# Two last stages of a graph and expert kernel become one: finding the picked rows and the last expert network, with a place of its own for every gathered tile

## The chip, the cores and the metric

The kernel runs on one core of a Trainium2 chip. The time is device time in microseconds (us) of one execution of the whole program; lower is better.

## The reference

The program runs two layers (graph convolution, attention mixing, expert network) over 12500 nodes of 256 features in float32. What matters here is the last step of the second layer. A router gives every node one number; the 6249 nodes with the largest numbers are picked, and only for them a two-layer network is computed, scaled by the router's number and added to x:

```
weights = (jnp.einsum('bsd,do->bso', x, wr) + br)[..., 0]
_, idx = jax.lax.top_k(weights, k)
sel_idx = idx[:, :kk]
sel = jnp.take_along_axis(x, sel_idx[:, :, None], axis=1)
h = jax.nn.gelu(jnp.einsum('bkd,dh->bkh', sel, w1) + b1)
y = jnp.einsum('bkh,hd->bkd', h, w2) + b2
w_sel = jnp.take_along_axis(weights, sel_idx, axis=1)
y = y * w_sel[..., None]
processed = jnp.zeros_like(x).at[batch_idx, sel_idx].set(y)
return processed + x
```

`w1` is 256 x 1024 and `w2` 1024 x 256. The order of the picked nodes doesn't matter, since the result goes back to each node's own row.

## The kernel before, in words

Every stage is a function with its own semaphores and buffers, and a barrier of all engines at its end. There is no scheduler: each engine's instructions run in the order in which the code writes them, and semaphores join the engines. The last four stages are `normalize` (norm3), `select`, `pick_rows` and `ffn1`.

`norm3` writes, for each node, a row of 512 numbers to `pick_from` in HBM: the normalized x, and the x to which the result is added. `select` finds which nodes are picked (`g.picked`, a 128 x 100 map of 0 and 1) and their numbers (`g.gain`), while SyncE stores x itself to the output; it waits for that store before it ends.

`pick_rows` makes the list. The picked nodes are numbered 0 to 6248, in 49 tiles of 128 (`PICK_TILES`). TensorE counts how many are picked ahead of each column (`ps_a`, `ps_s`). For each tile, VectorE marks which column holds each of its 128 numbers (`mark`, four portions at `CUTS`: 13, 12, 12 and 12 tiles), TensorE fetches that column's running counts, gains and base by a product (`ps_rows`, six banks), and VectorE turns them into the row number and the gain (`find`: compare and sum, copy, multiply). At the end one addition writes `g.pick_row` for all tiles, and one reduction over 49 x 128 numbers writes `g.pick_gain`.

`ffn1` works on 25 groups of two tiles (`GROUP`, `ROWS` = 256 rows). For each tile GpSimd (POOL) gathers 128 rows of 512 numbers with one indirect DMA (`gather`, `rows`, six buffers, `LOADS`), and writes 128 result rows of 256 to the output with another (`scatter`, from `y`, six buffers). TensorE's order is written out: `turn(gi + 1)` (four transposes of the next group into `ps_t`), the first product of group gi (16 float32 matmuls, shown as 32 passes, into the four banks `ps_h`), then `last(gi - 1)` (two times eight float32 matmuls and one bias matmul into `ps_f`, line 3159). ScalarE applies the gelu into `ht`, VectorE copies the turned tiles to `xt` (`keep_turned`) and adds (`add`). The gather of tile t waits until the group whose buffer it takes has been added:

```
if t >= LOADS:
    pool.wait_ge(added, t // GROUP - LOADS // GROUP + 1)
```

so group gi is gathered once group gi - 3 has been added, which is behind `last(gi - 3)`; TensorE's next instructions are the transposes of group gi - 1. `b2.split` (lines 185 to 194) makes the bias of the second product out of three bfloat16 parts on VectorE, and TensorE waits for it before its first transpose.

`g.x_flat` is the buffer of x in SBUF, 128 partitions of 25600 numbers, which neither of the last two stages uses before the change.

## Time and profile before

| | |
|---|---|
| time, median of 3 runs | 8606.35 us |
| lowest and highest | 8606.04 and 8610.86 us |
| span of the profiled execution, first to last instruction | 8601.4 us |
| median time less that span | 4.95 us |
| TensorE matmul busy, whole span | 6543.5 us (76%) |
| finding stage, first GpSimd instruction | 7944.25 us |
| expert stage, first transpose | 8022.32 us |
| expert stage, last bias matmul starts | 8587.67 us |

The profile gives the profiled execution as a span; no separate time of that execution is given, so the difference to the median stands for what lies around a span. All starts are microseconds from the span's start. PE is TensorE, PEld its weight loads, DVE VectorE, ACT ScalarE, POOL GpSimd, SP SyncE. A float32 matmul shows as two passes. The granted clock is a share of full speed: 1.00 is 2.4 GHz, 0.50 is 1.2 GHz.

### The profile page before, as it was taken

The numbers are of one execution on the slowest core, as the hardware profiler recorded it, in microseconds if no ns is written. First come the engines' busy times: TensorE is split into PE (matmuls) and PEld (weight loads), VectorE is DVE, ScalarE is ACT, GpSimd is POOL, SyncE is SP. The second block draws the span as 40 slices with busy tenths as digits, with TensorE's granted clock in tenths as the row PEclk, the third lists the DMA queues.
The fourth block names the chain that finished last, engine by engine and source line by source line (L and its number), as shares of the span: only waits on it lengthen the run. The fifth ranks groups of instructions, "written<-read, shape, count | busy, mean of one in ns | idle before, by whom it ended". The sixth has DMA issues, their size and how long they took to land. (4 is left out here: it accounts for less than half of the span.)

```text
span 8601.4 us, 109803 instructions
## 1 busy us (share of the span) xinstructions
PE 6543.5 (76%) x28541; PEld 4878.9 (57%) x28542; DVE 3556.7 (41%) x8183; ACT 1914.3 (22%) x4350; POOL 3828.7 (45%) x3997
## 2 busy tenths in 40 slices
PE   3797877887777899466688878771888776986677
PEld 2555555555547677443466656561666565766566
DVE  3211123333334222433355555547666555776200
ACT  1123420000001122111122222220123344661111
POOL 1567777777772000277677777761000000003111
PEclk9898878888875999578799998895999998995888
DMA  5776779999972000467677777762777665645110
GB/s 163 252 240 221 231 244 342 342 340 339 338 242 90 28 21 21 132 213 236 219 242 248 243 240 241 237 221 71 249 235 230 209 201 179 202 161 179 40 33 29
DMA packets 604940, 1708.05 MB, mean 199 GB/s; under 512 B 109370, under 2 KB 334479, under 8 KB 515140
## 3 DMA queue, kind: packets, MB, share of 16 engines
q1 hardware_dynamic: 338260, 981.33, 33.2%
q0 software_dynamic: 190752, 655.07, 24.0%
q10 hardware_dynamic: 75764, 69.93, 2.7%
q8 instruction: 45, 0.74, 0.0%
q14 instruction: 119, 0.97, 0.0%
HBM read 1084.38 MB, written 624.00 MB: 199 GB/s over the span
## 5 line engine op out<-in xcount | busy, mean ns | idle before, releaser
L723 POOL DMA_INDIRECT rows_ring<-h_rows,src_idx x1660 | 1730.5, 1042 | 651.0 <-issue 505.2
L1839 POOL DMA_INDIRECT x_sb<-xn_rows,src_tile x1563 | 1524.8, 976 | 473.4 <-issue 449.0
L816 PE MATMUL agg_ps_sum<-agg_rows,agg_sel_w 128*128 128x257 f32 x3080 | 1005.7, 475 | 266.0 <-DMA agg_rows<-edge_rows 183.7
L2610 PE MATMUL sums_ps_sum<-x_sb,sums_weighted 128*125 x4124 | 995.3, 397 | 264.2 <-DVE sums_weighted L2574 179.6
L2610 PEld LDWEIGHTS sums_ps_sum<-x_sb,sums_weighted 128*125 128x125 f32 x4124 | 780.5, 194 | 478.9 <-issue 355.3
L2574 DVE SCALAR_TENSOR_TENSOR sums_weighted<-x_sb 128x125 f32 x2062 | 720.5, 349 | 532.3 <-PE sums_ps_sum L2610 385.6
L816 PEld LDWEIGHTS agg_ps_sum<-agg_rows,agg_sel_w 128*128 128x128 f32 x3080 | 537.8, 219 | 509.4 <-issue 372.2
L792 DVE TENSOR_TENSOR agg_sel<-iota,dst_item 128x1280 bf16<-128x1280 f32 x166 | 250.6, 1509 | 881.0 <-PE agg_ps_sum L817 878.2
L2540 POOL DMA_INDIRECT node_tops<-tops,last_edge x98 | 93.4, 953 | 1118.4 <-DMA x_sb<-row_lots 1100.7
L2131 PE MATMUL mix_ps_h<-mix_x1t,mix_w 128*128 128x256 f32 x1600 | 386.7, 397 | 0.7 <-ACT mix_x1t L2193 0.7
L2642 ACT ACTIVATE sums_z<-sums_ps_sum 125x257 f32<-125x257 f32 x500 | 192.5, 385 | 857.8 <-PE sums_ps_sum L2610 771.5
L2140 PE MATMUL mix_ps_f<-mix_w,mix_ht 128*128 128x256 f32 x1600 | 372.1, 386 | 0.9 <-ACT mix_ht L2178 0.9
L2131 PEld LDWEIGHTS mix_ps_h<-mix_x1t,mix_w 128*128 128x128 f32 x1600 | 328.9, 206 | 54.6 <-ACT mix_x1t L2193 0.9
L2140 PEld LDWEIGHTS mix_ps_f<-mix_w,mix_ht 128*128 128x128 f32 x1600 | 295.9, 190 | 70.2 <-issue 32.9
L850 ACT ACTIVATE x_sb<-agg_ps_sum 128x256 f32 (+1 forms) x98 | 37.6, 383 | 1316.4 <-PE agg_ps_sum L817 1316.4
L575 POOL TENSOR_TENSOR x_sb<-x_sb,norm_xn 128x512 f32 (+1 forms) x50 | 64.0, 1280 | 578.3 <-DVE norm_xn L539 578.3
L1589 POOL IOTA sets_set_i<- 128x501 int32 x1 | 0.6, 552 | 675.5 <-POOLq L114 675.5
L817 PE MATMUL agg_ps_sum<-ones_bf,agg_sel 128*128 128x1 bf16 x1660 | 290.3, 175 | 0.0
L3117 POOL DMA_INDIRECT ffn_rows<-pick_from,pick_row x50 | 48.5, 970 | 491.4 <-DVE ffn_y L3211 426.6
L794 DVE TENSOR_TENSOR agg_sel_w<-agg_sel,w_item 128x1280 f32<-128x1280 bf16 x166 | 247.8, 1493 | 20.2
L2092 PE MATMUL mix_ps_q<-mix_xt,mix_wq 128*128 128x256 f32 x400 | 143.5, 522 | 127.6 <-DMA mix_xt<-xn_turned 126.0
L3173 PE MATMUL ffn_ps_h<-ffn_xt,ffn_w 128*128 128x256 f32 x800 | 230.9, 460 | 0.0
(547 smaller groups left out, 11321.3 us busy)
## 6 DMA issues: line engine op xcount, KB each, us to landing
row_lots<-x_sb SPq DMA_DIRECT2D x195, 1048.0 KB
x_sb<-row_lots SPq DMA_DIRECT2D x195, 1048.0 KB
edge_rows<-rows_ring POOLq DMA_DIRECT2D x154, 1290.0 KB
agg_rows<-edge_rows SPq DMA_DIRECT2D x154, 1290.0 KB
sums<-sums_z ACTq DMA_DIRECT2D x500, 125.5 KB
fin_z<-sums SPq DMA_DIRECT2D x97, 642.5 KB, 3.8
xn_turned<-norm_xt SPq DMA_DIRECT2D x150, 256.0 KB, 2.1
rows_ring<-h_rows,src_idx POOLq DMA_INDIRECT x1660
```

The source lines that it names most:

```text
L723: pool.indirect_dma_start(self.ring[:, s, i, :], None, self.table, bass.IndirectOffsetOnAxis(g.src_idx[:, item:item + 1], 0)).then_inc(sel ...
L792: dve.tensor_tensor(sel[:, u, :, :], places, dst, ALU.is_equal).then_inc(eq_done, 1)
L794: dve.tensor_tensor(sel_w[:, u, :, :], sel[:, u, :, :], w, ALU.mult).then_inc(sel_ready, 1)
L816: pe.matmul(ps[:, bass.ds(off, W)], sel_w[:, u, j, :], tiles[:, j, 0:W], start=False, stop=False, skip_group_check=True)
L817: pe.matmul(ps[:, bass.ds(off + W, 1)], sel[:, u, j, :], g.ones_bf[:, 0:1], start=False, stop=False, skip_group_check=True).then_inc(item_ ...
L1839: pool.indirect_dma_start(self.ring[:, s, i, :], None, g.xn_rows, bass.IndirectOffsetOnAxis(g.src_tile[:, tile:tile + 1], 0)).then_inc(sel ...
L2131: mm = pe.matmul(ps_h[i][:, m % 2, :], w1[:, c, m * P:(m + 1) * P], x1t[:, c, :], start=(c == 0), stop=(c == KC - 1))
L2140: pe.matmul(ps_f[:, j, :], ht[:, m, j * P:(j + 1) * P], w2[:, m, :], start=(m == 0), stop=False)
L2574: dve.scalar_tensor_tensor(weighted[:, s + j, :, :], nodes[:, bass.ds(base, SET)].unsqueeze(2).to_broadcast([P, SET, WEIGHTS]), flat_cols[ ...
L2610: pe.matmul(ps[0:M, bass.ds(bank, SW)], weighted[:, s + j, :, :].rearrange("p n w -> p (n w)"), rows[:, bass.ds(off, SW)], start=False, st ...
L2642: act.activation(z[0:M, w, :], ps[0:M, u * BANK:u * BANK + SW], ACT.Copy).then_inc(sum_kept, 1)
L3173: mm = pe.matmul(ps_h[i][:, m % 2, :], w1[:, c, m * P:(m + 1) * P], chunk(xt, u, c), start=(c == 0), stop=(c == KC - 1))
```

## The change

`pick_rows` and `ffn1` become one stage, `pick_and_ffn1`.

- `rows` is no longer a ring of six buffers but a view of x's buffer with 50 places of 512 numbers, one for each gathered tile. `y` is gone: `add` writes its result over the second half of the gathered row, and `scatter` sends it from there. So `gather` waits for no `added`, and `add` for no `stored`.
- VectorE writes the row numbers portion by portion (`rows_set`), and GpSimd begins the gathers of a portion then. All scatters stand behind all 50 gathers.
- The counting row `slot_i` is as long as one portion, with four begins and ends in place of one, and `hot` has two halves.
- `find` sums the gain in its multiplication (`accum_out`); the closing reduction is gone.
- The six banks of the finding are the banks `ps_t` and `ps_h` of the expert part, and the weights are loaded from the start of the joint stage.

```diff
--- before.py
+++ after.py
@@ -2991,109 +2991,36 @@
                 dve.tensor_tensor(g.gain[:, :], w[:, :], g.picked[:, :], ALU.mult)
 
 
-def pick_rows(nc, g):
+def pick_and_ffn1(nc, g):
 
     T = TILES
-    SLOTS = PICK_TILES * P
+    M = FF // P
     CUTS = [0, 13, 25, 37, PICK_TILES]
-    BANKS = 6
+    CUT = max(b - a for a, b in zip(CUTS[:-1], CUTS[1:]))
...
-        slot_i = ph.sb("slot_i", [P, SLOTS], I32)
+        hot_ready, listed, taken, rows_set = ph.sem("hot_ready"), ph.sem("listed"), ph.sem("taken"), ph.sem("rows_set")
+        w_loaded, turned, x_kept, h_done, h_kept, f_done, added, stored = (
+            ph.sem(s) for s in ("w_loaded", "turned", "x_kept", "h_done", "h_kept", "f_done", "added", "stored"))
+        loaded = [ph.sem(f"loaded{gi}") for gi in range(PICK_GROUPS)]
+        slot_i = ph.sb("slot_i", [P, CUT * P], I32)
         rank_i = ph.sb("rank_i", [P, PICK_TILES], I32)
         rank = ph.sb("rank", [P, PICK_TILES])
         below = ph.sb("below", [P, P])
         total = ph.sb("total", [P, 1])
         begin = ph.sb("begin", [P, 1])
-        end = ph.sb("end", [P, 1])
...
+        begins = ph.sb("begins", [P, len(CUTS) - 1])
+        ends = ph.sb("ends", [P, len(CUTS) - 1])
         table = ph.sb("table", [P, 2 * P + 1])
-        hot = ph.sb("hot", [P, SLOTS])
+        hot = ph.sb("hot", [P, 2, CUT * P])
...
-                mark(CUTS[0], CUTS[1])
-                for i in range(1, len(CUTS)):
-                    if i + 1 < len(CUTS):
-                        mark(CUTS[i], CUTS[i + 1])
-                    for t in range(CUTS[i - 1], CUTS[i]):
-                        find(t)
-                dve.wait_ge(taken, PICK_TILES)
-                dve.tensor_tensor(g.pick_row[:, 0:PICK_TILES], base[:, :], at[:, :], ALU.add)
-                dve.tensor_reduce(g.pick_gain[:, 0:PICK_TILES], gains[:, :, :], AX, ALU.add)
...
-    LOADS = 6
...
-        rows = ph.sb("rows", [P, LOADS, 2 * C])
+        gains = ph.sb("gains", [P, 2, P])
+        rows = g.x_flat.rearrange("p (t c) -> p t c", c=2 * C)
+        assert rows.shape[1] == ALL_PICKS
...
-        y = ph.sb("y", [P, LOADS, C])
...
+        ps_a = ps_f[0][:, :, :].rearrange("p j c -> p (j c)")
+        ps_s = ps_f[1][:, :, :].rearrange("p j c -> p (j c)")
+        lists = [t[:, :, :].rearrange("p a b -> p (a b)") for t in ps_t + ps_h]
+        BANKS = len(lists)
...
+                pool.iota(slot_i[:, :], pattern=[[1, CUT * P]], base=0, channel_multiplier=0).then_inc(iotas, 1)
+                pool.iota(rank_i[:, :], pattern=[[P, PICK_TILES]], base=0, channel_multiplier=1).then_inc(iotas, 1)
+
                 def gather(t):
-                    s = t % LOADS
-                    if t >= LOADS:
-                        pool.wait_ge(added, t // GROUP - LOADS // GROUP + 1)
-                    pool.indirect_dma_start(rows[:, s, :], None, g.pick_from, bass.IndirectOffsetOnAxis(g.pick_row[:, t:t + 1], 0)).then_inc(loaded[s], 16)
+                    pool.indirect_dma_start(rows[:, t, :], None, g.pick_from, bass.IndirectOffsetOnAxis(g.pick_row[:, t:t + 1], 0)).then_inc(loaded[t // GROUP], 16)
 
                 def scatter(t):
-                    s, m = t % LOADS, (P if t < PICK_TILES - 1 else PICK_TAIL)
+                    m = P if t < PICK_TILES - 1 else PICK_TAIL
                     pool.wait_ge(added, t // GROUP + 1)
-                    pool.indirect_dma_start(g.out, bass.IndirectOffsetOnAxis(g.pick_row[0:m, t:t + 1], 0), y[0:m, s, :], None,
-                                            bounds_check=NODES - 1, oob_is_err=False).then_inc(stored[s], 16)
-
-                for t in range(PICK_GROUPS * GROUP):
-                    gather(t)
-                    if t >= LOADS and t % GROUP == 1:
-                        scatter(t - LOADS - 1)
-                        scatter(t - LOADS)
-                for t in range(PICK_GROUPS * GROUP - LOADS, PICK_TILES):
+                    pool.indirect_dma_start(g.out, bass.IndirectOffsetOnAxis(g.pick_row[0:m, t:t + 1], 0), rows[0:m, t, C:2 * C], None,
+                                            bounds_check=NODES - 1, oob_is_err=False).then_inc(stored, 16)
+
+                for i, (t0, t1) in enumerate(zip(CUTS[:-1], CUTS[1:])):
+                    pool.wait_ge(rows_set, i + 1)
+                    for t in range(t0, t1 if t1 < PICK_TILES else ALL_PICKS):
+                        gather(t)
+                for t in range(PICK_TILES):
                     scatter(t)
-                for s in range(LOADS):
-                    pool.wait_ge(stored[s], 16 * len(range(s, PICK_TILES, LOADS)))
+                pool.wait_ge(stored, 16 * PICK_TILES)
 
             @block.tensor
             def _(pe):
+                pe.wait_ge(counted, 1)
+                pe.matmul(ps_a[0:T, 0:P], g.picked[:, :], below[:, :], start=True, stop=True)
+                pe.matmul(ps_a[0:T, P:2 * P], g.gain[:, :], g.ident[:, :], start=True, stop=True).then_inc(first_done, 1)
+                pe.wait_ge(counted, 2)
+                pe.matmul(ps_s[0:T, 0:1], g.upper[0:T, 0:T], total[0:T, :], start=True, stop=True).then_inc(starts_done, 1)
+                for i, (t0, t1) in enumerate(zip(CUTS[:-1], CUTS[1:])):
+                    pe.wait_ge(hot_ready, i + 1)
+                    for t in range(t0, t1):
+                        if t >= BANKS:
+                            pe.wait_ge(taken, t + 1 - BANKS)
+                        pe.matmul(lists[t % BANKS][:, 0:2 * P + 1], hot[0:T, i % 2, (t - t0) * P:(t - t0 + 1) * P], table[0:T, :], start=True, stop=True).then_inc(listed, 1)
...
+                pe.wait_ge(taken, PICK_TILES)
 
                 def turn(gi):
                     u = gi % 2
                     if gi >= 2:
                         pe.wait_ge(x_kept, gi - 1)
+                    pe.wait_ge(loaded[gi], 16 * GROUP)
                     for j in range(GROUP):
                         t = gi * GROUP + j
-                        pe.wait_ge(loaded[t % LOADS], 16 * (t // LOADS + 1))
                         for c in range(KC):
-                            mm = pe.transpose(ps_t[u][:, c, j * P:(j + 1) * P], rows[:, t % LOADS, c * P:(c + 1) * P], g.ident[:, :])
+                            mm = pe.transpose(ps_t[u][:, c, j * P:(j + 1) * P], rows[:, t, c * P:(c + 1) * P], g.ident[:, :])
...
+                done(dve.tensor_copy(begin[0:T, :], ps_s[0:T, 0:1]))
+                for i, t0 in enumerate(CUTS[:-1]):
+                    op = dve.tensor_scalar(begins[0:T, i:i + 1], begin[0:T, :], float(t0 * P), None, ALU.subtract)
+                done(op)
+                done(dve.tensor_scalar(ends[0:T, :], begins[0:T, :], total[0:T, 0:1], None, ALU.add))
+                done(dve.tensor_scalar(table[0:T, 0:P], ps_a[0:T, 0:P], begin[0:T, 0:1], None, ALU.add))
+
+                def mark(i):
+                    part = slice(0, (CUTS[i + 1] - CUTS[i]) * P)
+                    done(dve.tensor_scalar(hot[0:T, i % 2, part], slot_i[0:T, part], begins[0:T, i:i + 1], None, ALU.is_ge))
+                    dve.scalar_tensor_tensor(hot[0:T, i % 2, part], slot_i[0:T, part], ends[0:T, i:i + 1], hot[0:T, i % 2, part], ALU.is_lt, ALU.mult).then_inc(hot_ready, 1)
+
+                def find(t):
+                    got = lists[t % BANKS]
+                    dve.wait_ge(listed, t + 1)
+                    done(dve.tensor_scalar(junk[:, t % 2, :], got[:, 0:P], rank[:, t:t + 1], 0.0, ALU.is_le, ALU.add, accum_out=at[:, t:t + 1]))
+                    dve.tensor_copy(base[:, t:t + 1], got[:, 2 * P:2 * P + 1])
+                    dve.scalar_tensor_tensor(gains[:, t % 2, :], g.iota[:, :], at[:, t:t + 1], got[:, P:2 * P], ALU.is_equal, ALU.mult,
+                                             accum_out=g.pick_gain[:, t:t + 1]).then_inc(taken, 1)
+
+                mark(0)
+                for i, (t0, t1) in enumerate(zip(CUTS[:-1], CUTS[1:])):
+                    if i + 2 < len(CUTS):
+                        mark(i + 1)
+                    for t in range(t0, t1):
+                        find(t)
+                    dve.wait_ge(taken, t1)
+                    dve.tensor_tensor(g.pick_row[:, t0:t1], base[:, t0:t1], at[:, t0:t1], ALU.add).then_inc(rows_set, 1)
...
-                        s = t % LOADS
-                        if t >= LOADS:
-                            dve.wait_ge(stored[s], 16 * (t // LOADS))
-                        op = dve.scalar_tensor_tensor(y[:, s, :], ps_f[gi % 2][:, j, :], col(g.pick_gain, t), rows[:, s, C:2 * C], ALU.mult, ALU.add)
+                        op = dve.scalar_tensor_tensor(rows[:, t, C:2 * C], ps_f[gi % 2][:, j, :], col(g.pick_gain, t), rows[:, t, C:2 * C], ALU.mult, ALU.add)
...
-        lambda: pick_rows(nc, g),
-        lambda: ffn1(nc, g),
+        lambda: pick_and_ffn1(nc, g),
```

On GpSimd, at the end of its program, before the change (`ffn_rows` is the ring, `out_dram` the output, and a wait in brackets names whatever the reused semaphore was called first; here it is `added`):

```order
L3022 IOTA pick_slot_i 128x6272
L3023 IOTA pick_rank_i 128x49
L3019 UNCONDITIONAL_BRANCH
L113 ISA [waits barrier_Pool_Activation_PE_DVE_SP_gather]
L3111 UNCONDITIONAL_BRANCH [waits barrier_Pool_Activation_PE_DVE_SP_gather]
L3117 DMA ffn_rows<-pick_from,pick_row 128x512 x6
L3117 DMA ffn_rows<-pick_from,pick_row 128x512 [waits items_rows_ready] x2
L3122 DMA out_dram<-ffn_y,pick_row 12500x256 [waits items_rows_ready] x2
L3117 DMA ffn_rows<-pick_from,pick_row 128x512 [waits items_rows_ready] x2
L3122 DMA out_dram<-ffn_y,pick_row 12500x256 [waits items_rows_ready] x2
```

And GpSimd after it (`x_sb` is now the gathered rows; the wait on the gathers is `rows_set`, that on the scatters `added`):

```order
L3044 IOTA pick_slot_i 128x1664
L3045 IOTA pick_rank_i 128x49
L3048 DMA x_sb<-pick_from,pick_row 128x512 [waits items_tables]
L3048 DMA x_sb<-pick_from,pick_row 128x512 x12
L3048 DMA x_sb<-pick_from,pick_row 128x512 [waits items_tables]
L3048 DMA x_sb<-pick_from,pick_row 128x512 x11
L3048 DMA x_sb<-pick_from,pick_row 128x512 [waits items_tables]
L3048 DMA x_sb<-pick_from,pick_row 128x512 x11
L3048 DMA x_sb<-pick_from,pick_row 128x512 [waits items_tables]
L3048 DMA x_sb<-pick_from,pick_row 128x512 x12
L3053 DMA out_dram<-x_sb,pick_row 12500x256 [waits norm0_var_ready] x49
```

Before, two gathers and two scatters took turns, each behind a wait for an addition; now 50 gathers stand together behind four waits for row numbers, and the 49 scatters follow.

On VectorE, where the finding of the last tile ends and the bias begins, before:

```order
L3070 TENSOR_SCALAR pick_junk,pick_at<-pick_ps_rows,pick_rank 128x128
L3071 COPY pick_base<-pick_ps_rows 128x1
L3072 SCALAR_TENSOR_TENSOR pick_gains<-iota,pick_at,pick_ps_rows 128x128
L3081 TENSOR_TENSOR pick_row<-pick_base,pick_at 128x49
L3082 TENSOR_REDUCE pick_gain<-pick_gains 128x49
L3019 UNCONDITIONAL_BRANCH
L3192 UNCONDITIONAL_BRANCH
L185 COPY ffn_b_rest<-ffn_b_given 3x256
L188 CAST ffn_b_cut<-ffn_b_rest 3x256
```

And after:

```order
L3168 TENSOR_SCALAR pick_junk,pick_at<-pick_ps_t,pick_rank 128x128
L3169 COPY pick_base<-pick_ps_t 128x1
L3170 SCALAR_TENSOR_TENSOR pick_gains,pick_gain<-iota,pick_at,pick_ps_t 128x128
L3180 TENSOR_TENSOR pick_row<-pick_base,pick_at 128x12
L185 COPY pick_b_rest<-pick_b_given 3x256
L188 CAST pick_b_cut<-pick_b_rest 3x256
```

The reduction and the change of stage between the finding and the bias are gone, the multiplication has a second output, and the row numbers of the last portion alone are written there (the other three additions stand at the ends of their portions).

TensorE's own order is the same instructions in the same order, without the change of stage between them.

## Rows read from the trace of the kernel before

**Rows 1.** The head of the page.

```profile
span 8601.4 us, 109803 instructions
```

**Rows 2.** Waits, 8025 to 8560 us: who waited, total us, times, longest.

```profile
PE ffn_ps_t L3148 <- DMA ffn_rows<-pick_from,pick_row: 120.2, 44, 4.8
```

**Rows 3.** The chain that ended last, one group: start, us, what.

```profile
8424.59 0.22 PE ffn_ps_f L3159
...
8425.99 0.39 POOL ffn_rows L3117
...
8427.28 3.48 DMA ffn_rows<-pick_from,pick_row
...
8430.80 0.69 PE ffn_ps_t L3148 x2
8431.49 9.65 PE ffn_ps_h L3173 x32
...
8448.45 0.22 PE ffn_ps_f L3159
```

**Rows 4.** The same chain, the start of the expert stage.

```profile
8022.32 1.94 PE ffn_ps_t L3148 x8
8024.27 8.62 PE ffn_ps_h L3173 x32
8032.89 0.44 PE ffn_ps_t L3148 x4
8033.33 6.91 PE ffn_ps_h L3173 x32
```

**Rows 5.** The same chain, the last group.

```profile
8565.53 7.10 PE ffn_ps_h L3173 x32
...
8580.16 3.65 PE ffn_ps_f L3158 x16
...
8587.67 0.23 PE ffn_ps_f L3159
```

**Rows 6.** Stretches: length, each engine's busy us, granted clock, DMA share, GB/s.

```profile
3000.00:3400.00 400.00, 400.00 (x1835) 289.61 (x1833) 88.98 (x189) 88.04 (x222) 0.00 (x0) 1.00 0.07 21
...
8033.00:8048.00 15.00, 14.76 (x69) 12.24 (x67) 0.89 (x2) 4.12 (x10) 0.00 (x0) 1.00 0.00 1
...
8431.50:8437.00 5.50, 5.50 (x14) 4.33 (x14) 0.69 (x1) 0.84 (x2) 0.00 (x0) 0.51 0.05 19
```

The five busy times of a row are those of PE, PEld, DVE, ACT and POOL.

**Rows 7.** Timeline of the finding: start, us, engine, line, operation, idle before it.

```profile
7944.25 5.35 POOL L3022 IOTA pick_slot_i<- 128x6272 int32 x1 [95.88 <-ACTq L3019]
...
7945.22 0.63 PE L3029 MATMUL pick_ps_a<-ident,gain 128*100 128x128 f32 x2
...
7949.78 0.19 DVE L3053 CAST pick_rank<-pick_rank_i 128x49 f32<-128x49 int32 x1 [4.85 <-POOL pick_rank_i L3023]
...
7957.94 0.34 DVE L3070 TENSOR_SCALAR_CACHE_REDUCE pick_junk<-pick_ps_rows,pick_rank 128x128 f32<-128x128 f32 x1
...
7958.33 0.16 DVE L3071 COPY pick_base<-pick_ps_rows 128x1 f32<-128x1 f32 x1
7958.41 0.34 DVE L3072 SCALAR_TENSOR_TENSOR pick_gains<-iota,pick_at,pick_ps_rows 128x128 f32<-128x128 f32 x1
7958.66 0.34 DVE L3070 TENSOR_SCALAR_CACHE_REDUCE pick_junk<-pick_ps_rows,pick_rank 128x128 f32<-128x128 f32 x1
...
7997.68 0.34 DVE L3072 SCALAR_TENSOR_TENSOR pick_gains<-iota,pick_at,pick_ps_rows 128x128 f32<-128x128 f32 x1
...
7998.18 6.68 DVE L3082 TENSOR_REDUCE pick_gain<-pick_gains 128x49 f32<-128x6272 f32 x1
...
8018.72 0.28 DVE L185 COPY ffn_b_rest<-ffn_b_given 3x256 f32<-3x256 f32 x1 [13.86 <-DMA ffn_b_given<-in_L_ffn_b_dram]
```

**Rows 8.** Two lines of another stage: ns least/median/most, first and last start us.

```profile
L1970 DVE TENSOR_SCALAR ctx_low<-ctx_kb x50: 426/427/635, 3746.6 to 4174.5; 128x512 f32<-128x512 f32 x50
...
L1839 POOL DMA_INDIRECT x_sb<-xn_rows,src_tile x1563: 942/946/1462, 3731.6 to 5779.8; - x196
```

More of the change, by code:

```diff
@@ L2991, in _ @@
                 dve.tensor_tensor(g.gain[:, :], w[:, :], g.picked[:, :], ALU.mult)
-def pick_rows(nc, g):
+def pick_and_ffn1(nc, g):
     T = TILES
-    SLOTS = PICK_TILES * P
+    M = FF // P
     CUTS = [0, 13, 25, 37, PICK_TILES]
-    BANKS = 6
+    CUT = max(b - a for a, b in zip(CUTS[:-1], CUTS[1:]))
+    ALL_PICKS = PICK_GROUPS * GROUP
     with phase(nc, "pick") as ph:
         iotas, step, counted, first_done, starts_done = (ph.sem(s) for s in ("iotas", "step", "counted", "first_done", "starts_done"))
-        hot_ready, listed, taken = ph.sem("hot_ready"), ph.sem("listed"), ph.sem("taken")
-        slot_i = ph.sb("slot_i", [P, SLOTS], I32)
+        hot_ready, listed, taken, rows_set = ph.sem("hot_ready"), ph.sem("listed"), ph.sem("taken"), ph.sem("rows_set")
[3 more added lines that the diff above has]
+        slot_i = ph.sb("slot_i", [P, CUT * P], I32)
         rank_i = ph.sb("rank_i", [P, PICK_TILES], I32)
@@ L3085, in ffn1 @@
-def ffn1(nc, g):
-    M = FF // P
-    LOADS = 6
-    with phase(nc, "ffn1") as ph:
-        w_loaded, turned, x_kept, h_done, h_kept, f_done, added = (
-            ph.sem(s) for s in ("w_loaded", "turned", "x_kept", "h_done", "h_kept", "f_done", "added"))
-        loaded = [ph.sem(f"loaded{s}") for s in range(LOADS)]
-        stored = [ph.sem(f"stored{s}") for s in range(LOADS)]
-        rows = ph.sb("rows", [P, LOADS, 2 * C])
+        gains = ph.sb("gains", [P, 2, P])
+        rows = g.x_flat.rearrange("p (t c) -> p t c", c=2 * C)
@@ L3193, in _, with done @@
             def _(dve):
+                n = Count()
+                def done(op):
+                    op.then_inc(step, 1)
+                    dve.wait_ge(step, n.up())
+                done(dve.tensor_tensor(below[:, :], g.upper[:, :], g.ident[:, :], ALU.add))
+                dve.sem_inc(counted, 1)
+                dve.memset(g.pick_row[:, PICK_TILES:], 0)
+                dve.memset(g.pick_gain[:, PICK_TILES:], 0.0)
+                dve.tensor_scalar(table[:, 2 * P:2 * P + 1], g.part[:, :], float(P), None, ALU.mult)
@@ new lines, in _ @@
+                dve.wait_ge(iotas, 2)
+                dve.tensor_copy(rank[:, :], rank_i[:, :])
+                dve.wait_ge(first_done, 1)
+                done(dve.tensor_copy(total[0:T, :], ps_a[0:T, P - 1:P]))
+                dve.sem_inc(counted, 1)
+                dve.tensor_copy(table[0:T, P:2 * P], ps_a[0:T, P:2 * P])
+                dve.wait_ge(starts_done, 1)
+                done(dve.tensor_copy(begin[0:T, :], ps_s[0:T, 0:1]))
+                for i, t0 in enumerate(CUTS[:-1]):
+                    op = dve.tensor_scalar(begins[0:T, i:i + 1], begin[0:T, :], float(t0 * P), None, ALU.subtract)
```

52 lines of the change are left out of this document (removed).

## The prediction

> **What bounds the kernel now.** I read the page first, then the chain that ended last, then the waits and the timeline of the last two stages, because every other stage is untouched. The span is 8601.4 us [rows 1]; the median of the runs shown is 8606.35, 4.95 above it. I keep that 4.95 as it is, and the whole change lies after 7944 us.
>
> The expert stage runs from its first transpose at 8022.32 [rows 4] to the end of its last bias matmul, 8587.67 + 0.23 = 8587.90 [rows 5]: 565.58 us for 25 groups of two tiles. The reader should look at one group in the middle [rows 3]. A bias matmul of the last product (L3159) starts at 8424.59 and the same one a group later at 8448.45, so a group takes 23.86 us. In between the chain leaves TensorE: VectorE adds, GpSimd issues the gather of two tiles whose buffers have just come free, the transfer lands, and only at 8430.80 do the last two transposes run. TensorE is the bound for the rest of the group. It waits 120.2 us for these gathers in 44 waits [rows 2], which is two for each of 22 groups.
>
> The stall has a second price. Just behind such a stall TensorE's granted clock is 0.51 although it is busy all the time, that is 1.2 GHz; where two groups follow each other without a stall it is 1.00, 2.4 GHz [rows 6]. So the 32 matmul passes of the first product take 9.65 us behind a stall [rows 3], and 6.91 where there was none [rows 4].
>
> Ahead of the expert stage TensorE does nothing useful between the finding and 8022.32: VectorE reduces the gains until 7998.18 + 6.68 = 8004.86, the next stage starts loading its weights, and VectorE's first bias operation at 8018.72 sat idle 13.86 us for the bias [rows 7].
>
> **The change part by part: the start.** Counted on VectorE's own chain, up to its first bias operation, since TensorE's first transposes follow it.
>
> - The counting row for the slots shrinks from 6272 to 1664 elements. It takes 5.35 us, and VectorE idles 4.85 us until the two iotas are done [rows 7]. 5.35 x 1664/6272 = 1.42, so 3.9 less. TensorE's first counts, which it covered, end at 7945.22 + 0.63 = 7945.85 [rows 7], and the two iotas now end at 7944.25 + 1.42 + 0.2: no new wait behind them. -3.9.
> - Four small subtractions instead of one addition: a one-column copy is 0.16 us long [rows 7], and the four run behind each other with one wait. +0.4 (0.2 to 0.6).
> - 49 multiplications now also sum their rows. That form is not in the trace, but the comparison next to it sums too: its start at 7957.94, the copy behind it at 7958.33, so 0.39 from start to start; the multiplication without a sum takes 7958.66 - 7958.41 = 0.25 [rows 7]. The bounds are nothing, if the sum is formed on the way, and the difference, 0.14: 0 to 6.9 us for 49. The comparison also has a wait behind it that the multiplication doesn't have, so I stay somewhat below the upper row and take 0.10, +4.9. A tile, 7958.66 - 7957.94 = 0.72 now, is then 0.82.
> - Three more small additions for the row numbers, each with a wait for the last find: by the one there is, 7998.18 - 7997.68 = 0.50 from the last multiplication over it to the reduction [rows 7], against 0.25, so 0.25 x 3 = +0.75.
> - The reduction over all gains, 6.68 us, is gone, and so is the stage's end with its barrier.
> - The loads of the weights start at 7944 with nothing else on the DMA queues. They are 60 us early, so the wait of 13.86 is gone.
>
> VectorE's first bias operation was at 8018.72. It comes at 7998.18 - 3.9 + 0.4 + 4.9 + 0.75 = 8000.3. From it to the first transpose were 8022.32 - 8018.72 = 3.6 us, and they stay. The first transpose is at 8003.9: **-18.4 us**.
>
> **Gathers and finding together.** POOL has nothing to do but 50 gathers, 8427.28 - 8425.99 = 1.29 us from one to the next [rows 3]. The first find starts one tile ahead of the row at 7957.94, less 3.5 and 13 take 13 x 0.82, so the first portion is known at 7964.5, and the 50 gathers end near 7964.5 + 50 x 1.29 = 8029. TensorE wants a group, two tiles, every 15 us, from 8004 on, and POOL issues two in 2.6 us. The first 13 tiles have landed by 7964.5 + 16.8 + 3.5 = 7985. Gathers would have to be six times slower before TensorE waited, so this is priced at nothing; if that cover were gone, a group would wait as in [rows 3]. All scatters now stand behind all gathers on POOL, first at 8029; nobody waits for a scatter but the stage's end, and two scatters take 2.6 us of a 15 us group. The last one comes the same distance behind the last matmul as now.
>
> What could collide is VectorE and GpSimd, which now work at the same time: two marks of the finding and four copies and casts of the bias lie in the time of the gathers. In another stage 50 multiplications of 512 elements from SBUF to SBUF ran in the time of 0.95 us gathers: 426 ns least, 427 median, 635 most [rows 8]. So a collision cost at most 0.21 us, and half of them cost nothing. For seven such operations this gives 0 to 1.5 us; I take 0, since the median shows none.
> The Trainium skill ("SBUF — State Buffer", section "Who interferes with whom") states that a VectorE copy, cast or tensor_scalar in its two-port mode and GpSimd's descriptor writing hold a shared port pair exclusively, and that the loser waits for the whole instruction. By that rule each of the seven could wait for a whole gather. The trace does not agree: 0.21 us is the longest delay in 50, where a whole gather is 0.95.
>
> **The expert stage.** Every tile has a place of its own, so no gather waits for an addition and no addition for a scatter. What TensorE then does per group without a stall is read where the trace has it. The last group without its transposes: 8580.16 - 8565.53 = 14.63, which is 7.10 for the first product and 7.53 for the second [rows 5]. The four transposes of an unstalled group: 0.44 [rows 4]. Together 15.07 us. The other conditions of TensorE's queue (a bank of the first product free, the hidden rows kept, the sum taken) were met in [rows 4, 5] without a wait: in 15 us without a stall ScalarE is busy 4.12 us and VectorE 0.89 [rows 6].
>
> - The two first pairs of transposes, cold: 1.94. The first product of group 0, cold: 8.62 [rows 4]. Both stay, since TensorE is idle for 4 us ahead of them as well.
> - Groups 1 to 24: 24 x 15.07 = 361.7, less 0.44 for the last, which has no transposes ahead, less 0.19 for the first, whose product follows no bias matmul (7.10 against 6.91).
> - The last second product: 8587.90 - 8580.16 = 7.74 [rows 5].
>
> Sum 1.94 + 8.62 + 361.7 - 0.63 + 7.74 = 379.4 against 565.6: **-186.2 us**. Some 120 of it are waits and the rest is clock and the slower transposes.
>
> Total -204.6: span 8396.8, time 8606.35 - 204.6 = 8401.8. I say **8402 us**, 2.4% faster.
>
> **The rivals.**
>
> A. *The stalls go but the clock does not come back.* Every group begins at 1.2 GHz for some reason other than the gather. Then the first product stays at 9.65 (+2.55 over 7.10) and the four transposes stay at 2 x 0.69 [rows 3] for 0.44, +0.94: 3.5 a group, 24 x 3.5 = +84, so 8486. Against it: another stage, the first layer's expert network, was busy on TensorE for 400.00 of 400.00 us and had clock 1.00 [rows 6]; and 15 us without a stall had 1.00 in this stage.
>
> B. *Slower: TensorE stays at 1.2 GHz through the stage*, held down rather than let up by uninterrupted work. Everything in it takes twice as long: 2 x 379.4 - 565.6 - 18.4 = +175, 8781. It decides from the point where more than (565.6 + 18.4 - 379.4) / 379.4 = 54% of the work is done at the low clock. Nothing speaks for it; the same window at 1.00 speaks against.
>
> C. *VectorE and GpSimd block each other for whole instructions.* Seven operations wait 0.95 us each for a gather, on the way to the first transpose: +6.7, 8408. The longest delay of 0.21 us in [rows 8] speaks against. This is what the page's rule quoted above would do.
>
> D. *The gathers are late in spite of their head start*, since each moves 256 KB and they now follow each other without a pause. If each took 3.5 us (its landing in [rows 3]) with none beside another, two would take 7 of 15 us and nothing changes. At 8 us a tile TensorE would wait about 1 us a group, +25, 8427. I find no row with such a rate.
>
> **How the numbers follow.** The forecast has 0.86, A 0.05, B 0.02, C 0.04, D 0.03. The forecast's own bounds are: the sums in 49 multiplications 0 to 6.9 for 4.9, collisions to +1.5, and the period of a group 14.88 (0.44 + 6.91 + 7.53, with the first product of [rows 4]) to 15.2, so -5 and -5 below, +2, +1.5 and +3 above; with 2 to 4 us between runs of the kernel before (8606.04 to 8610.86) this is 8394 to 8413 (not all at once). The range reaches on over C and into D: 8392 to 8426. What a measurement can tell from no change is about 0.2%, 17 us. Faster by more than that: all but B and something unseen, 0.97; same 0.01; slower 0.02.
>
> **What the profile of the changed kernel should show.** First transpose near 8004, first gather near 7965, the last near 8029, the reduction gone. No wait of a transpose for a gather in the list of waits. A first product of 32 passes in 6.9 to 7.1 us in all groups but the first, clock 1.00 from group 1 on, successive L3159-like bias matmuls 15.1 us apart. Last addition near 8383. The prediction is wrong if the groups' period is over 15.5, if finding takes more than 0.86 us a tile, or if the bias operations take much over 3.6 us.

## The result, and the profile after

| | before | after |
|---|---|---|
| time, median of 4 runs | 8608.3 us | 8395.69 us |
| lowest and highest | 8606.04 and 8610.86 | 8392.08 and 8400.41 |
| ratio, 95% interval | | 0.9754 (0.974 to 0.9768) |
| last stages: start to first transpose | 78.05 us | 55.20 us |
| first transpose to end of last bias matmul | 565.58 us | 377.42 us |
| from there to the span's end | 13.50 us | 13.76 us |

The profiled execution of the changed kernel took 8392.08 us and its span is 8390.3 us. The last stages begin with their first VectorE instruction, at 7943.92 us, 0.35 earlier than before (7944.27). The three rows at the foot of the table give -22.85, -188.16 and +0.26, with the 0.35 together -211.1, which is all of 8601.4 - 8390.3. While the last eight experiments ran, the kernel before took 11044 and 11033 us, so of those eight only times inside the last stages are read.

The chain that ended last, from the last row numbers on; the columns are start, us, what:

```profile
7995.37 0.17 DVE pick_row L3180
7995.54 0.20 DVE pick_b_rest L185
7995.77 0.36 DVE pick_b_cut L188
...
7998.49 0.48 DVE pick_b_parts L194
...
7999.12 1.94 PE pick_ps_t L3089 x8
8001.06 7.80 PE pick_ps_h L3114 x32
...
8023.53 0.21 PE pick_ps_f L3100
8023.74 0.59 PE pick_ps_t L3089 x4
8024.32 6.91 PE pick_ps_h L3114 x32
...
8034.90 3.65 PE pick_ps_f L3099 x16
8038.55 0.21 PE pick_ps_f L3100
```

The last row is the same bias matmul one group later. Against [rows 3] nothing stands between the bias matmul and the transposes any more: no addition, no GpSimd, no transfer. A group takes 8038.55 - 8023.53 = 15.02 us for 23.86, and the first product 6.91 for 9.65. There is no row for the one of [rows 2]; over the same stretch the transposes never wait for a gather. The list of waits, 7999 to 8385 us, has only these for TensorE's transposes, both ahead of the first of them (who waited, for whom, total us, times, longest):

```profile
PEld pick_ps_t L3089 <- issue: 7.8, 1, 7.8
PE pick_ps_t L3089 <- DVEq L195: 7.4, 1, 7.4
```

The gathers, all 50 of them (least/median/most ns of one, first and last start, landing):

```profile
L3048 POOL DMA_INDIRECT x_sb<-pick_from,pick_row x50: 942/946/2248, 7963.5 to 8027.7; - x50
...
DMA to landing us min/median/max: 3.4/3.7/4.4
```

The longest of them, 2.25 us, stands beside one of VectorE's marks (the timeline of all engines, other rows left out):

```profile
7974.83 1.01 DVE L3162 TENSOR_SCALAR pick_hot<-pick_slot_i,pick_begins 100x1536 f32<-100x1536 int32 x1
7975.87 1.82 DVE L3163 SCALAR_TENSOR_TENSOR pick_hot<-pick_slot_i,pick_ends,pick_hot 100x1536 f32<-100x1536 int32 x1
7976.26 2.25 POOL L3048 DMA_INDIRECT x_sb<-pick_from,pick_row  x1 [0.30 <-issue]
```

Five of the 50 take longer than 0.96 us: 1.50 (at 7963.48), 1.52 (7965.29), 1.34 and 2.25 beside the marks of the third and fourth portion, and 1.08 (7996.31) beside the operations on the bias. Why the prediction was right, below, comes back to it.

Stretches of the expert part, columns as in [rows 6]:

```profile
8009.40:8024.40 15.00, 15.00 (x72) 12.55 (x71) 1.26 (x3) 3.70 (x9) 11.34 (x13) 1.00 0.73 212
8024.40:8378.00 353.60, 352.13 (x1636) 294.03 (x1634) 34.37 (x71) 77.25 (x184) 50.63 (x52) 1.00 0.06 22
```

The granted clock is 1.00 from the second group on, even while the gathers still move 212 GB/s. The finding, on VectorE's timeline:

```profile
7945.58 0.19 DVE L3147 CAST pick_rank<-pick_rank_i 128x49 f32<-128x49 int32 x1 [1.01 <-POOL pick_rank_i L3045]
...
7946.67 0.34 DVE L3155 TENSOR_SCALAR pick_begins<-pick_begin 100x1 f32<-100x1 f32 x4
...
7953.46 0.34 DVE L3168 TENSOR_SCALAR_CACHE_REDUCE pick_junk<-pick_ps_t,pick_rank 128x128 f32<-128x128 f32 x1
...
7953.93 0.34 DVE L3170 SCALAR_TENSOR_TENSOR pick_gains<-iota,pick_at,pick_ps_t 128x128 f32<-128x128 f32 x1
7954.19 0.08 DVE L3170 DVE_READ_ACCUMULATOR pick_gains<-iota,pick_at,pick_ps_t 128x1 f32 x1
7954.19 0.34 DVE L3168 TENSOR_SCALAR_CACHE_REDUCE pick_junk<-pick_ps_t,pick_rank 128x128 f32<-128x128 f32 x1
```

The multiplication that sums has a second row, the reading of the sum, but the next comparison starts at the same time as that reading. A tile takes 7954.19 - 7953.46 = 0.73 us, for 0.72 in [rows 7].

### The profile page after: what moved, and what is told of

Its sections match the earlier page's. It is cut to its first block and busy times, and to the rows that moved or that the text cites. A ratio compares the mean times of both kernels' runs of the same rounds, so it can differ in the third digit from the quotient of the medians.

```text
span 8390.3 us, 109810 instructions
## 1 busy us (share of the span) xinstructions
PE 6473.1 (77%) x28541; PEld 4831.1 (58%) x28542; DVE 3545.2 (42%) x8238; ACT 1915.5 (23%) x4350; POOL 3823.0 (46%) x3997
## 5 line engine op out<-in xcount | busy, mean ns | idle before, releaser
L1924 PE MATMUL ctx_ps_kv<-ctx_wkv,ctx_xt 128*128 128x512 f32 x400 | 225.9, 718 | 0.7 <-DMA ctx_xt<-xn_turned 0.6
L2178 ACT ACTIVATE mix_ht<-mix_ps_h,mix_b 128x256 f32<-128x256 f32 x400 | 164.9, 470 | 254.2 <-PE mix_ps_h L2131 254.1
```

What stands on the lines that cost most here:

```text
L1924: mm = pe.matmul(ps[u][j][:, :], chunk(xt, u, c, j), wkv[:, c, :], start=(c == 0), stop=(c == KC - 1))
```

## The experiments

The twelve runs are of ten kernels, since two were run twice. All give times for the whole program; their traces are also read inside the last stages ("local": from the stage's first VectorE instruction), where the kernel before has 657.1 us in all and the changed one 446.4. The first four ran with runs of the kernel before at 8606.33 us (median of 16, 8592.04 to 8686.22). Of the other eight, from other_stall on, only local times are used. The changed kernel itself was not run beside these eight. Where an edit leaves the expert part alone, it takes there what it takes in the changed kernel (weights_late 377.4 us, reduced 378.3 and 378.5, for 377.4), so the expert part can be compared; the finding can't be, where gathers run beside it (last section).

**Which part brings the gain: six buffers, eight, fifty.**

```diff
ring8 (before)
-    LOADS = 6
+    LOADS = 8
places_only (before, two stages kept)
...
-        rows = ph.sb("rows", [P, LOADS, 2 * C])
...
-        y = ph.sb("y", [P, LOADS, C])
...
+        rows = g.x_flat.rearrange("p (t c) -> p t c", c=2 * C)
...
joint_ring6 (after, with the ring and its waits put back)
+    LOADS = 6
...
+                    if t >= LOADS:
+                        pool.wait_ge(added, t // GROUP - LOADS // GROUP + 1)
```

Expected of ring8: 

> The kernel before with a ring of eight buffers instead of six, nothing else. My theory: the gain of the expert stage comes from the gathers being a group earlier, not from the places in x's buffer or from the joint stage. The gather of group gi then waits for group gi - 4, so no transpose waits for a gather, the first product is back at 7.1 us and a group takes 15.0 us instead of 23.9: about 188 us faster than before, 8420. Rival (one group of lead isn't enough, only all gathers ahead are): most of the 120 us of waits stay and the time is above 8500.

Expected of places_only: 

> The kernel before with its two stages and its reduction, but 50 places in x's buffer, all gathers ahead of all scatters. My theory: the expert stage as in the changed kernel (377 us instead of 566), the start as before (first transpose near 8022): 188 us faster, 8420, the same as with a ring of eight. Rival (places and joint stage need each other): less than 150 us.

Expected of joint_ring6: 

> The changed kernel, joint stage, gathers by portions, but with six places used in turn and the waits for additions and stores of before. My theory: the first transpose near 7999 as in the changed kernel, the stall of 6 us in 22 groups and the low clock behind it as before: 23 us faster than before, 8585. Rival (the joint stage itself brings more than the start): under 8560.

| | time (lowest to highest) | ratio to before | local |
|---|---|---|---|
| ring8 | 8416.72 (8394.53 to 8428.32) | 0.9766 (0.9715 to 0.9817) | 470.1 |
| places_only | 8413.62 (8408.11 to 8426.93) | 0.9763 (0.9712 to 0.9814) | 470.1 |
| joint_ring6 | 8583.64 (8568.65 to 8593.34, and one of ten 9320.29) | 0.9968 (0.9945 to 0.999) | 630.6 |

`LOADS` sets both rings, so ring8 has two more buffers in `rows` (256 KB each) and two more in `y` (128 KB each). Its waits over 290 us of the expert stage:

```profile
DVE ffn_y L3211 <- PE ffn_ps_f L3159: 257.4, 19, 13.6
...
POOL ffn_rows L3117 <- DVE ffn_y L3211: 182.3, 18, 10.1
```

GpSimd still waits for every addition before it gathers, and it costs nothing: with a group more of distance no transpose waits, and a group takes what it takes in the changed kernel, 8236.40 - 8221.38 = 15.02 us on its chain:

```profile
8221.38 0.21 PE ffn_ps_f L3159
...
8222.18 6.91 PE ffn_ps_h L3173 x32
...
8236.40 0.21 PE ffn_ps_f L3159
```

Two buffers more in each ring are worth as much as the 50 places, 657.1 - 470.1 = 187.0 us. The joint stage by itself is worth 657.1 - 630.6 = 26.5 us, of which 22.9 are the start (first transpose at local 55.2) and 3.8 the expert part, whose price for a stall differs from group to group (next experiment). 187.0 + 26.5 = 213.5 against 210.7 for both.

**How much of the gain is clock.** The kernel before, with ten float32 matmuls of 256 columns whose result nobody uses put into TensorE's queue ahead of the transposes of each group from the fourth on, to fill the stall. The gathers stay as late as they were.

```diff
filled_stall (before)
+                    if gi >= 3:
+                        for _ in range(10):
+                            pe.matmul(ps_t[u][:, 0, :], w1[:, 0, 0:P], w1[:, 0, 0:ROWS], start=True, stop=True)
```

> The kernel before, with ten float32 matmuls of 256 columns (20 passes, some 4.3 us at full clock) of unused data ahead of the transposes of groups 3 to 24, where TensorE waits for the gather. They write a bank that the transposes then overwrite. The waits for the gathers stay, only TensorE's clock is kept up. My theory of two prices: the first product falls from 9.65 to about 7.1 us and the transposes a little, 22 x 2.4 + 22 x 0.4 = about 60 us faster than before, 8548, granted clock near 1.0. Rival (the clock is a symptom and costs nothing, or the work added delays the transposes): same as before or slower.

8543.37 us (8538.83 to 8608.86), ratio 0.9914 (0.9887 to 0.9942); local 601.2, that is 55.9 less than before. One group of its chain:

```profile
8424.78 3.51 DMA ffn_rows<-pick_from,pick_row
...
8428.34 0.44 PE ffn_ps_t L3151 x2
8428.77 6.91 PE ffn_ps_h L3176 x32
...
8445.69 3.47 DMA ffn_rows<-pick_from,pick_row
...
8449.20 0.44 PE ffn_ps_t L3151 x2
8449.64 6.91 PE ffn_ps_h L3176 x32
```

The transfer is on the chain as it was, but the product behind it takes 6.91 and the granted clock there is 1.00 (8449.7 to 8456). The group takes 8449.20 - 8428.34 = 20.86 us. So of 23.86 - 15.02 = 8.84 us that the group of [rows 3] lost to its late gather, 3.0 were the lower clock and 5.84 the wait. That group is one of the dearest. In the kernel before the first product behind a stall takes 7.98 to 9.65 us, with the clock over it from 0.87 (8148.2 to 8156) down to 0.72 (8431.5 to 8441); two that follow each other on its chain:

```profile
8124.45 9.57 PE ffn_ps_h L3173 x32
...
8148.12 7.99 PE ffn_ps_h L3173 x32
```

Here 21 of the 22 such products take 6.91 (the last 8.60). Over all 22 groups the low clock cost 55.9 / 22 = 2.5 us each. The profiled execution is the one of 8608.86 us: its last stages start at 8005.8 us for 7944.3, so what it has over the median lies ahead of them, where the two kernels are the same. Useless work in a stall made this kernel 0.9% faster.

**The other direction: a stall that has nothing to do with gathers.** The changed kernel, whose transposes from the fourth group on wait until the scatters of the group three before have landed.

```diff
other_stall (after)
                     pe.wait_ge(loaded[gi], 16 * GROUP)
+                    if gi >= 3:
+                        pe.wait_ge(stored, 16 * GROUP * (gi - 2))
```

> The changed kernel with one wait added: TensorE's transposes of group gi wait until the scatters of group gi - 3 have landed, which is about as long behind the last addition as a gather was before. No gather is late. My theory: any pause of 5 to 6 us per group costs itself and the low clock behind it: period near 24 us, about 200 us slower than the changed kernel, 8595. Rival (the low clock before came from the gathers' traffic, not from the pause): first product stays at 7.1 us, period 20 to 21 us, 130 us slower.

Local: the expert part takes 550.3 us for 377.4, +173, somewhat below the expectation. From its chain:

```profile
10845.98 0.22 PE pick_ps_f L3102
...
10849.21 2.44 DMA out_dram<-x_sb,pick_row
...
10851.78 1.09 PE pick_ps_t L3091 x4
10852.87 8.71 PE pick_ps_h L3116 x32
...
10868.90 0.22 PE pick_ps_f L3102
```

A group takes 22.92 us: 5.58 of idle TensorE (10851.78 - 10845.98 - 0.22), 0.50 more in the transposes and 1.80 more in the first product, the clock being 0.80 over that product (10853 to 10861.5) and 1.00 behind it. 5.58 + 0.50 + 1.80 = 7.88, and 22 groups of it are 173. This group lies near the mean. The first products behind a stall go from 7.76 to 9.44 us here too:

```profile
10626.08 7.78 PE pick_ps_h L3116 x32
...
10670.96 9.21 PE pick_ps_h L3116 x32
```

So a stall of another origin costs clock as well, and nearly as much: 2.3 us a group on the mean, against 2.5 for the late gathers. Why the clock comes back sooner in one group than in the next, in both kernels, is open.

**The start of the stage: four edits.**

```diff
weights_late (after)
+                sp.wait_ge(rows_set, len(CUTS) - 1)
                 load_all(sp, w_loaded, ...
reduced (after; gains holds all tiles again)
-                                             accum_out=g.pick_gain[:, t:t + 1]).then_inc(taken, 1)
+                dve.tensor_reduce(g.pick_gain[:, 0:PICK_TILES], gains[:, :, :], AX, ALU.add)
split_late (after; pe.wait_ge(b2.ready, 1) moves to last(0) too)
-                dve.wait_ge(w_loaded, 64)
-                b2.split(dve, g)
+                    if gi == 0:
+                        dve.wait_ge(w_loaded, 64)
+                        b2.split(dve, g)
base_by_matmul (split_late, and)
+                        pe.matmul(ps_f[i % 2][:, 0, t:t + 1], hot[...], table[0:T, 2 * P:2 * P + 1], start=True, stop=True).then_inc(listed, 1)
...
-                    dve.tensor_copy(base[:, t:t + 1], got[:, 2 * P:2 * P + 1])
...
```

Expected of weights_late: 

> The changed kernel, but SyncE loads the weights only when all row numbers are written. My theory: the bias lands some 13 us after that instead of being there, so the first transpose comes near 8012.5 instead of 7999.1: 13.4 us slower than the changed kernel, 8409, and up to 10 more if the loads share the DMA engines with the gathers. Rival (the early loads hide nothing): same.

From the last row numbers to the first transpose it takes 10510.76 - 10492.50 = 18.26 us, for 7999.12 - 7995.37 = 3.75 in the changed kernel: +14.5. The early load is worth what the old wait for the bias was, 13.86 [rows 7].

Expected of reduced: 

> The changed kernel, but the gains are kept for all tiles and reduced at the end as before, and the multiplication doesn't sum. The trace of the changed kernel says that the sum costs 0.01 us a tile, since the accumulator's read lies under the next operation: then this is 6.7 - 0.5 = 6.2 us slower than the changed kernel. By the price of the prediction (0.10 us a tile) it would be 6.7 - 4.9 = 1.8 us slower.

Its second run: 

> The changed kernel with one part undone: the multiplications of the finding don't sum, and one reduction over 49 x 128 numbers follows the last row numbers (6.68 us before). By the trace of the changed kernel the sum in a multiplication costs 0.01 us (a tile takes 0.73 with it, 0.72 without), so the first transpose comes 6.68 - 0.5 = 6.2 us later and the time is about 6 us more. By the price of the prediction, 0.10 each, it is 6.68 - 4.9 = 1.8 us more.

Both runs agree to 0.2 us. In the first portions a comparison follows the last one every 0.72, 0.72, 0.71 us, against 0.73, 0.73, 0.72 in the changed kernel: the sum costs 0.01 us each, 0.5 us in all. The reduction's place in its chain:

```profile
10108.43 0.17 DVE pick_row L3179
10108.60 6.60 DVE pick_gain L3180
...
10118.93 1.94 PE pick_ps_t L3089 x8
```

10118.93 - 10108.43 = 10.50 against 3.75, +6.75, less 0.5: undoing that part costs 6.2 us by the rows, as was expected from the trace, and not the 1.8 of the prediction's price.

Expected of split_late: 

> The changed kernel, with the three bfloat16 parts of the second product's bias made on VectorE behind the copies of the first two turned groups, and TensorE waiting for them only at its first second product. They stood between the last row numbers (7995.5) and the first transpose (7999.1), 3.6 us on the chain; TensorE's first second product comes some 16 us later, so they have cover there. If that is what holds the first transpose, it comes 3.6 us earlier, and the time is 3.6 us less than the changed kernel's, about 8392. Rival: the first transpose is held by its own gather or by the last find, then nothing changes; the gathers of its group landed 25 us earlier, so I don't expect that.

The end of its finding on the timeline:

```profile
10268.47 0.17 DVE L3181 TENSOR_TENSOR pick_row<-pick_base,pick_at 128x12 uint32<-128x12 f32 x1
...
10268.54 1.94 PE L3088 MATMUL pick_ps_t<-ident,x_sb 128*128 128x128 f32 x8 [2.82 <-issue]
```

The first transpose now starts 0.07 us behind the row numbers for 3.75, so the bias was all that held it until then, and the copies and casts find cover later. But the first product took 8.46 for 7.80 there (its finding ran another way, see the last section), so the gain of a whole run is not measured; the rows give 3.7 us.

Expected of base_by_matmul: 

> As split_late, and VectorE's copy of the base (0.08 us a tile on its chain) is gone: TensorE fetches the 49 bases by a product of one column each into a bank of their own, from which the addition of the row numbers reads them. If VectorE is what bounds the finding, a tile takes 0.65 for 0.73, the first transpose comes another 3.9 us earlier, and the time is about 7.5 less than the changed kernel's, 8388. Rival: TensorE becomes the bound: two passes of 257 columns take 0.60 us at 1.2 GHz, and two more passes of one column, each with a weight load of 0.2 ahead of it that it can't hide, make 1.0 us a tile, 13 us more instead.

The rival came. VectorE's timeline, two tiles of its first portion:

```profile
10372.43 0.35 DVE L3170 TENSOR_SCALAR_CACHE_REDUCE pick_junk<-pick_ps_h,pick_rank 128x128 f32<-128x128 f32 x1 [0.53 <-PE pick_ps_f L3077]
...
10373.71 0.35 DVE L3170 TENSOR_SCALAR_CACHE_REDUCE pick_junk<-pick_ps_h,pick_rank 128x128 f32<-128x128 f32 x1 [0.53 <-PE pick_ps_f L3077]
```

A tile takes 1.28 us at a granted clock of 0.50 (10369.5 to 10383), TensorE being busy all the time. It takes 0.66 in stretches of the later portions, though the clock is 0.50 there too (10405.3 to 10411): those tiles follow a mark, during which TensorE could work ahead into free banks. VectorE's part alone would have been 0.66 throughout. The rival had 1.0 us a tile, with 0.60 for the two wide passes at 1.2 GHz; 0.60 is their time at clock 1.00 (2.40 us for four tiles in the changed kernel, 7972.3 to 7974.7), and at 0.50 they took 1.00 of the 1.28. The last comparison comes at local 83.2 us for 76.8 in split_late, both with the idle stretches of the last section in it, so the price over all tiles is not measured.

**Gathers only when all is found.**

```diff
gathers_late (after)
-                    pool.wait_ge(rows_set, i + 1)
+                    pool.wait_ge(rows_set, len(CUTS) - 1)
```

> The changed kernel, but no gather starts before all row numbers are written. My theory: TensorE's start needs only the first four tiles; these land at about 7995.5 + 4 x 1.29 + 3.7 = 8004.4, while the bias is ready at 7999.1, so the start is 3 to 5 us later and nothing after it changes: 3 to 5 us slower. If VectorE and GpSimd hinder each other while both work, the finding here is shorter, by at most 1 us. Rival (the start portion by portion is worth a portion's time or more): over 10 us slower.

Second run: 

> The changed kernel, but GpSimd begins all gathers only when the row numbers of all four portions are there, at 7995.5 instead of 7963.0. The first group's two gathers then land at about 7995.5 + 1.3 + 3.7 = 8000.5 and the later ones 2.6 us a group, against 15 us that TensorE takes: first transpose 1.5 us later, the copies and casts of the bias beside gathers as before, +1 to +5 us in all. Rival: the portions are what makes the head start, without them the second and third group are late, the clock is lost again for some groups, and it costs over 10 us. Had the finding been slowed by gathers beside it, a tile of it would now take less than 0.73.

Local, the first transpose is at 56.9 and 57.0 us for 55.2 in the changed kernel, the finding as long as there (last comparison at 50.7 twice, for 50.6). The first product starts at 60.7 in both for 57.1, since its second tile's gather is waited for as well (1.7 us): +3.6, within the 1 to 5 expected. The expert part took 424.3 and 425.6, +47 and +48, but by the rows the rest of it is no late gather. TensorE, first groups of the second run:

```profile
10448.88 5.13 PE L3114 MATMUL pick_ps_h<-pick_xt,pick_w 128*128 128x256 f32 x23
10455.64 0.38 PE L3114 MATMUL pick_ps_h<-pick_xt,pick_w 128*128 128x256 f32 x1 [1.63 <-issue]
10462.87 2.08 PE L3114 MATMUL pick_ps_h<-pick_xt,pick_w 128*128 128x256 f32 x4 [6.85 <-issue]
```

TensorE stops in the middle of a product, waiting for nothing that the profile shows, up to the end of the gathers (last section). Whether the late gathers would have cost more than the 3.6 us without that stays open. The gathers themselves, none of them beside a mark now:

```profile
L3048 POOL DMA_INDIRECT x_sb<-pick_from,pick_row x50: 942/946/1087, 10431.7 to 10493.3; - x50
```

## Why the prediction was right

8402 was forecast, 8395.69 measured, in the range. By its own steps:

- **The expert stage**, forecast 379.4, measured 377.4. The period of a group was read at 15.07 and is 15.02 (24 x 0.05 = 1.2). That it came so near is partly luck: the first product is 6.91 and not 7.10, the four transposes are 0.59 and not 0.44, and the two nearly cancel. The cold first product took 7.80 instead of 8.62 (0.8), which is luck too: in filled_stall, which leaves that start as it was, it took 8.22. That a group without a stall keeps 2.4 GHz was taken from a pair of groups in the trace of before, and held for all. Rivals A and B fell with the first product's 6.91 and the clock of 1.00.
- **"Some 120 of it are waits and the rest is clock and the slower transposes"** left 66 us for that rest. filled_stall, which leaves the waits and takes the low clock away, gives 55.9. The wait was undercounted: from the bias matmul to the last two transposes pass 8430.80 - 8424.81 = 5.99 us [rows 3], 132 over 22 groups, and 132 + 55.9 = 188. The 120.2 are the waits alone; the first two transposes of each group run between them.
- **What makes the gain** was put in one step, "every tile has a place of its own". It is right, but it hides how little is needed: ring8 has the whole gain of the expert stage with LOADS = 8. The 50 places bring nothing beyond it there.
- **The start**, forecast -18.4, measured -22.85. The iota and the subtractions were -3.5 together and came as -3.4 (first comparison 9.54 us behind the stage's start for 12.96). Reduction and weights were -6.68 and -13.86; between the last row numbers and the bias there were 20.7 us and there is 0.1. The term that was off is that of the 49 summing multiplications: +4.9, taken from the upper of two bounds because the comparison beside it seemed to pay 0.14 for its sum. Measured, 0.5, so it was sized 4.4 too high, and that is nearly all by which the start was missed. The 0.14 there are the wait behind it, for an instruction that needs the sum; an instruction that doesn't need it starts beside the reading. The lower bound was the better row.
- **Collisions**, priced at 0, bound 1.5: one cast took 0.35 us where the two like it took 0.28, and the third and fourth portions' marks took 1.01 and 1.82 us beside gathers, as the second's did before the gathers began. Rival C asked for 6.7. But the prediction looked at one side only: it was GpSimd that waited. The gather that starts at 7976.26 takes 2.25 us, 1.31 more than the usual 0.94, and the mark that had started 0.39 ahead of it ends 1.43 us behind the gather's start. The five long gathers lose 3.0 us against the median, and where no gather stands beside a mark (gathers_late) the longest takes 1.09. [Rows 8] have the sign of it, a gather of 1462 ns with a median of 946. It cost nothing because no transpose waits for a gather. The Trainium skill ("SBUF — State Buffer", section "Who interferes with whom") has a VectorE instruction in a two-port mode and GpSimd exclude each other: the one that issues first keeps the shared ports for its whole length, and the other waits. The trace agrees as far as GpSimd waits, with the 1.31 us above; which mode the marks ran in no row shows, and none shows a VectorE instruction that waited for a whole gather of 0.95 us.
- **Gathers beside finding and product**: first at 7963.5 (forecast 7964.5), last at 8027.7 (8029), landing in 3.4 to 4.4 us, none waited for. Rival D fell. The last start came right by two errors: gathers follow each other every 1.25 us and not 1.29, and the five long ones add 3.0.
- **The rest**: the span came 6.5 us below the forecast one (4.4 start, 2.0 expert part, 0.35 an earlier stage start, less 0.26). Around the span lie 1.8 us in the profiled execution, where 4.95 had been assumed from a median; that is why a figure that was 6.5 too high for the span is 9.7 too high for that execution (8401.8 against 8392.08).

## What to carry to other kernels

Where a ring's buffer comes free only after its group is finished, count how far ahead that lets the next transfer start, and try one group's worth of buffers more before rebuilding: here two more places in each ring gave 187 of 211 us. In this kernel a stall of 5.6 to 6.0 us on TensorE cost the wait and on the mean some two fifths as much again in clock (2.3 and 2.5 us), so a stall that can't be removed may be worth filling. Before moving work from the bound engine to one that looks idle, take that engine's time at its lower clock: for four tiles of the finding TensorE took 2.40 us at clock 1.00 (from 7972.33 in the changed kernel) but 3.63 at 0.50 (from 7967.78), VectorE takes 2.92, and two short passes more a tile made TensorE the bound. When two engines may exclude each other, read the durations of both.

## What the runs showed that was not expected

In the last eight runs TensorE and VectorE stood idle beside the gathers, for longer than in the changed kernel's own run. With gathers beside the finding, the last comparison came at local 72.9 us (reduced, both runs), 76.8 (split_late), 77.5 (weights_late), 78.1 (other_stall) and 83.2 (base_by_matmul), for 50.6 in the changed kernel's own run; without them it came at 50.7, twice (gathers_late). In gathers_late the same happened later, to the first product. Split_late's finding by stretches, columns as in [rows 6]:

```profile
10200.00:10210.00 10.00, 9.71 (x33) 5.56 (x31) 9.51 (x67) 0.00 (x0) 0.00 (x0) 0.93 0.00 0
...
10240.00:10268.00 28.00, 9.44 (x16) 4.18 (x16) 8.49 (x61) 0.00 (x0) 14.18 (x15) 0.50 0.55 157
```

In the second stretch no engine is busy for more than about half of it, the releasers that the profile names were long done, and the gathers move 157 GB/s; the changed kernel, with 212 GB/s, shows nothing of it in its own run. A late supply of instructions is a guess that nothing here supports: the profile's instruction queues moved one packet of 0.02 MB while TensorE stood in gathers_late_again (10455 to 10498) and four packets in the changed kernel's gathers (7963 to 8028), which tells neither for it nor against it. The cause stays open, and since the changed kernel was not run beside these eight, it is not known whether its own finding would have been as slow.
